# A two-pass chunk of the first layer, a bank shared by ScalarE and VectorE, a three-pass sum over d, and the late weights in 26 parts

## What is computed

```python
e = jnp.stack([tbl_0[ids[:, 0]], ..., tbl_38[ids[:, 38]]], axis=1)   # (1024, 39, 16)
x0 = xk = e
outs = []
for W in (f0, f1, f2):                         # (39*39,128), (128*39,128), (128*39,128)
    z = jnp.einsum('bfd,bgd->bfgd', x0, xk).reshape(b, f * g, d)
    xk = jnp.einsum('bpd,pm->bmd', z, W)       # x1, x2, x3
    outs.append(xk)
z = jnp.sum(jnp.concatenate(outs, axis=1), axis=-1)     # sum over d: r1, r2, r3
h = jnp.concatenate([z, dense_ctx], axis=1)             # 400 columns
h = jnp.maximum(h @ W_top1 + b_top1, 0.0)               # 512
h = jnp.maximum(h @ W_top2 + b_top2, 0.0)               # 256
y = h @ W_top3                                          # 1
```

## Time and profile before

| | us |
|---|---|
| median of 3 timed runs | 1279.11 |
| lowest and highest of them | 1278.82, 1797.93 |
| the profiled execution's own time | 1282.0 |
| its span, first to last instruction | 1279.9 |
| TensorE busy | 1244.3 (97%) |
| VectorE, GpSimd, ScalarE busy | 1056.1, 951.3, 752.1 |
| mean granted TensorE clock | 0.999 |

### The profile page before, as it was taken

The page is one execution under the profiler, slowest core; times in us unless marked ns, Lnnn a source line. Parts: engine busy times, 40 slices in busy tenths (PEclk is TensorE's granted clock), DMA queues, the critical chain, the costliest instruction groups (busy, mean ns, idle before and its releaser), DMA issues.

```text
span 1279.9 us, 19975 instructions
## 1 busy us (share of the span) xinstructions
PE 1244.3 (97%) x5517; PEld 969.6 (76%) x5517; DVE 1056.1 (83%) x3366; ACT 752.1 (59%) x2426; POOL 951.3 (74%) x844
## 2 busy tenths in 40 slices
PE   1989999999999999999999999999999999999999
PEld 0667778777787778777787777877787777877766
DVE  4778996988869997899878888699977989688882
ACT  4556664666646665566646666466655666566652
POOL 7668886788858886788867888588877888665650
PEclk9999999999999999999999999999999999999999
DMA  7542222122222212122211222222121222111000
GB/s 169 158 130 59 68 69 54 38 67 61 65 61 68 61 47 54 51 66 68 70 46 44 65 60 65 66 62 51 48 69 49 68 69 69 39 50 49 3 1 1
DMA packets 121764, 78.69 MB, mean 61 GB/s; under 512 B 77436, under 2 KB 89826, under 8 KB 121652
## 3 DMA queue, kind: packets, MB, share of 16 engines
q1 hardware_dynamic: 107418, 73.69, 20.4%
q0 software_dynamic: 10240, 2.64, 2.6%
q10 hardware_dynamic: 3994, 1.09, 0.4%
HBM read 18.50 MB, written 2.63 MB: 17 GB/s over the span
## 4 chain that ended last, share of the span: by engine, by line
PE 92%; SPq 3%; DMA 2%; POOL 1%; issue 1%; DVE 0%; ACT 0%
PE ps L510 22%; PE ps L514 22%; PE ps L511 22%; PE ps L490 13%; PE ps L537 6%; PE ps L526 5%; POOL x_in L404 1%; PE ps L602 1%; PE ps L473 1%; DMA x_rows<-x_in 1%; PE ps L614 1%; SPq L323 1%; DMA x_in<-in_tables,row_at 0%; SPq L377 0%; SPq L337 0%
## 5 line engine op out<-in xcount | busy, mean ns | idle before, releaser
L865 DVE SCALAR_TENSOR_TENSOR terms<-ps,x_scal,terms 128x128 f32<-128x128 f32 x2944 | 806.2, 342 | 158.4 <-ACT terms L692 94.1
L692 ACT ACTIVATE terms<-ps,x_scal 128x128 f32<-128x128 f32 x2048 | 583.7, 368 | 372.9 <-PE ps L514 366.0
L428 POOL TENSOR_TENSOR terms<-terms 128x1024 f32<-128x1024 f32 (+2 forms) x384 | 578.1, 1506 | 179.9 <-DVE terms L865 157.3
L510 PE MATMUL ps<-w_high,x_high 128*128 128x512 f32 (+1 forms) x1280 | 582.6, 455 | 4.7 <-DVE x_low L843 2.9
L514 PE MATMUL ps<-w_high,x_low 128*128 128x512 f32 (+1 forms) x1280 | 496.9, 388 | 0.0
L511 PE MATMUL ps<-w_low,x_high 128*128 128x512 f32 (+1 forms) x1280 | 495.1, 387 | 0.0
L404 POOL DMA_INDIRECT x_in<-in_tables,row_at x320 | 304.5, 951 | 81.7 <-issue 66.3
L510 PEld LDWEIGHTS ps<-w_high,x_high 128*128 128x128 f32 x1280 | 241.4, 189 | 85.0 <-issue 20.6
L511 PEld LDWEIGHTS ps<-w_low,x_high 128*128 128x128 f32 x1280 | 241.8, 189 | 77.7 <-issue 29.8
L514 PEld LDWEIGHTS ps<-w_high,x_low 128*128 128x128 f32 x1280 | 240.6, 188 | 50.4
L490 PE MATMUL ps<-prods,w 117*128 117x512 f32 x262 | 135.0, 600 | 5.2 <-DVE prods L831 4.9
(11 more groups left out here) (64 smaller groups left out, 446.8 us busy)
## 6 DMA issues: line engine op xcount, KB each, us to landing
prods<-x_cols SPq DMA_DIRECT2D x189, 234.0 KB
x_cols<-x_rows SPq DMA_DIRECT2D x96, 78.0 KB
x_first<-x_cols SPq DMA_DIRECT2D x95, 78.0 KB
x_in<-in_tables,row_at POOLq DMA_INDIRECT x320
x_diag<-x_scal SPq DMA_DIRECT2D x256, 9.8 KB
x_rows<-x_in SPq DMA_DIRECT2D x32, 80.0 KB, 2.4
s<-in_f SPq DMA_DIRECT2D x3, 832.0 KB, 11.7
wt<-in_W_top SPq DMA_DIRECT2D x1, 768.0 KB, 12.8
```

The source lines that it names most:

```text
L428: nc.gpsimd.tensor_tensor(t[:, 0:n], t[:, 0:n], t[:, n:2 * n], ALU.add).then_inc(s_tree, 1)
L510: nc.tensor.matmul(y, x1_high[:, par, at:at + P], high, start=True, stop=False)
L692: op = nc.scalar.activation(terms[:, u % 2, FB * ACT_BANKS.index(q) + i, :], ps[:, (BANKS * u + q) % RING, i * G:(i + 1) * G], ACT.Copy, s ...
L865: nc.vector.scalar_tensor_tensor(out=acc, in0=y, scalar=x0, in1=acc, op0=ALU.mult, op1=ALU.add).then_inc(s_mac, 1)
```

## The change

Six things change together. (1) The chunk with only two shifts (REST, now chunk 1; SHIFT_OF renames the shifts) is no longer multiplied in full precision. Its 78 rows of highs and, one third at a time, its two times 39 rows of lows lie together in `rest` (117 rows), and two float32r passes with two sets of weights (w0_rest) give what the three passes of a split chunk give. The lows get there by two transfers on ACT's queue (move_rest), the second only after the first pass has read the first. (2) Bank 2 is shared: ScalarE scales it in place in PSUM and VectorE adds all 512 columns to the running sums with one instruction (add_shared), in four chains in place of two. (3) The sum over d takes three float32r passes: x2 and x0 are split into highs and lows (split_x2_high on ACT, split_x2_low and split_scalars on DVE), and the diagonal is moved with both. (4) f2 and the MLP weights are loaded in 26 parts, four behind each group's diagonal, and group 0's diagonal goes out before group 1's rows. (5) In tiles 1 and 2 the passes over chunks are put in other slots, and chunks 5 and 4 change places (CIN1_OF). (6) In the tail the new splits stand among the MLP's.

```diff
+SHARED, ADD_AT = 2, 4
+SCALED_BANKS = tuple(sorted(ACT_BANKS + (SHARED,)))
-CHAINS = 2
+CHAINS = FB
+SHIFT_OF = (0, KT - 1) + tuple(range(1, KT - 1))
+REST, SPLIT = 1, (2, 3, 4)
+X2_HIGH, X2_LOW = 7, 8
+MOVE_LOWS = ((0, 8), (1, 3))
-CIN1 = ((0, 6), (1, 1), (1, 8), (2, 6), (2, 9), (3, 2), (3, 4))
+CIN1 = ((0, 6), (1, 3), (1, 9), (2, 1), (2, 4), (2, 8), (3, 1), (3, 4))
+CIN1_OF = (0, REST, REST, 2, 3, 5, 4, 6)
...
+        def move_rest(queue, i):
+            queue.dma_start(rest[KH:KR, :].bitcast(F32), prods_low[i * F:(i + 1) * F, 0, :].bitcast(F32)) \
+                .then_inc(s_rest, 16)
...
             def move_diag(gf, j):
-                sp.wait_ge(s_scal, gf + 1)
+                sp.wait_ge(s_scl, gf + 1)
                 sp.wait_ge(s_s3, gf * TILES - TILES + CREDIT_S3)
...
                 move_diag(gf, j)
+                for n in range((gf - 1) * 4, min(gf * 4, W2_PARTS + 13)):
+                    load_late(n)
...
+                elif k == REST:
+                    pe.wait_ge(s_wrest, 32)
+                    pe.wait_ge(s_rest, (gf - 1) * 32 + half * 16 + 16)
+                    passes = ((w0_rest[:, half, :], rest[:, :]),)
...
-                nc.tensor.matmul(ps[:, S3_BANK, 0:TB * FX], x2[:, u % 2, :],
-                                 x0_diag[:, j % 2, t].rearrange("p b f -> p (b f)"),
-                                 start=True, stop=True).then_inc(s_s3, 1)
+                nc.tensor.matmul(s3_sum, x2_high[:, :], high, start=True, stop=False)
+                nc.tensor.matmul(s3_sum, x2_high[:, :], low, start=False, stop=False)
+                nc.tensor.matmul(s3_sum, x2_low[:, :], high, start=False, stop=True).then_inc(s_s3, 1)
...
+                        y if q == SHARED else terms[:, u % 2, FB * ACT_BANKS.index(q) + i, :], y, ACT.Copy,
...
+            def split_x2_high(bt, u):
+                act.wait_ge(s_x2, bt * STEPS + u + CREDIT_X2)
+                act.wait_ge(s_s3, bt * STEPS + u - 1 + CREDIT_S3)
+                nc.scalar.activation(x2_high[:, :], x2[:, (u - 1) % 2, :], ACT.Copy).then_inc(s_x2h, 1)
...
+                    if front and now == MOVE_LOWS[0]:
+                        act.wait_ge(s_low, (gf - 1) * (NS + 1) + 1)
+                        move_rest(act, 0)
+                    if front and now == MOVE_LOWS[1]:
+                        act.wait_ge(s_cin1, gf * SLOTS + REST_SLOTS[0] + 1)
+                        move_rest(act, 1)
...
+            def add_shared(bt, u):
+                dve.wait_ge(s_ya, bt * (STEPS * NA) + scaled_through(BANKS * u + SHARED) + CREDIT_A)
+                dve.wait_ge(s_mac, bt * (STEPS * MACS) + added_through(BANKS * u + SHARED) - 1 + CREDIT_MAC)
+                acc = terms[:, u % 2, 0:FB, :].rearrange("p t g -> p (t g)")
+                nc.vector.tensor_tensor(acc, ps[:, (BANKS * u + SHARED) % RING, :], acc, ALU.add).then_inc(s_mac, 1)
```

More of the change, by code:

```diff
@@ L62 @@
 ACT_BANKS = (0, 3, 5, 7)
-NA = len(ACT_BANKS)
-DVE_BANKS = tuple(q for q in range(BANKS) if q not in ACT_BANKS)
-MACS = sum(min(FB, F - FB * q) for q in DVE_BANKS)
-CHAINS = 2
-TERMS = NA * FB
+SHARED, ADD_AT = 2, 4
+SCALED_BANKS = tuple(sorted(ACT_BANKS + (SHARED,)))
+NA = len(SCALED_BANKS)
+DVE_BANKS = tuple(q for q in range(BANKS) if q not in SCALED_BANKS)
+DVE_ORDER = tuple(k for q in DVE_BANKS for k in ((SHARED, q) if q == ADD_AT else (q,)))
+DVE_OPS = {q: 1 if q == SHARED else min(FB, F - FB * q) for q in DVE_ORDER}
+MACS = sum(DVE_OPS.values())
+CHAINS = FB
+TERMS = len(ACT_BANKS) * FB
 W1_CHUNKS = 3
@@ L331, in move_diag, with put_diag @@
+            def put_diag(j):
+                for b in range(TB):
+                    at = slice(b * D, (b + 1) * D)
+                    sp.dma_start(x0_diag[at, j % 2, :, :, b, 0:F].bitcast(F32), x0_hl[at, :, :, :].bitcast(F32)) \
+                        .then_inc(s_diag[j % 2], 16)
             def move_diag(gf, j):
[L333 removed]
+                sp.wait_ge(s_scl, gf + 1)
                 sp.wait_ge(s_s3, gf * TILES - TILES + CREDIT_S3)
[L335 to L338 removed]
+                put_diag(j)
@@ L340, in move_seconds @@
             def move_seconds(gf, j):
-                for k in range(1, KT):
-                    sp.wait_ge(s_cin1, gf * KT - KT + k + 1)
-                    move_second(sp, k, j)
+                for n in range(1, SLOTS):
+                    sp.wait_ge(s_cin1, gf * SLOTS - SLOTS + n + 1)
+                    if n != REST_SLOTS[0 if gf == 1 else 1]:
+                        move_second(sp, CIN1_OF[n], j)
             def next_cols(gf, j):
@@ L488, in cin1 @@
                     passes = ((w0[:, k, :], prods[0:KR, k, :]),)
-                for n, (w, x) in enumerate(passes):
-                    mm = nc.tensor.matmul(ps[:, X1_BANK, :], w, x, start=(k == 0 and n == 0),
-                                          stop=(k == KT - 1 and n == len(passes) - 1))
+                for i, (w, x) in enumerate(passes):
+                    mm = nc.tensor.matmul(ps[:, X1_BANK, cols], w, x, start=(k == 0 and i == 0),
+                                          stop=(n == SLOTS - 1 and i == len(passes) - 1))
                 mm.then_inc(s_cin1, 1)
@@ L555, in prologue @@
                 pe.wait_ge(s_denl, len(DENSE_BANKS))
-                for k in range(KT):
-                    cin1(0, k, True)
-                pe.wait_ge(s_w0h, NS)
-                pe.wait_ge(s_w0l, NS)
+                for n in range(SLOTS):
+                    cin1(0, n, True)
+                pe.wait_ge(s_w0h, NS + 1)
+                pe.wait_ge(s_w0l, NS + 1)
                 pe.wait_ge(s_w1h, len(W1_PIECES))
@@ L906, in step @@
                     if q in DVE_BANKS:
+                        if q == ADD_AT:
+                            add_shared(bt, u)
                         mac(bt, u, q)
+                    if q == X2_LOW and bt + u > 0:
+                        split_x2_low(bt, u)
+                    if front and now == SPLIT_SCALARS:
+                        split_scalars(gf, j)
                     if front and now in PRODUCTS:
```

196 lines of the change are left out of this document (133 added, 63 removed).

## The result

The changed kernel takes 1260.04 us (median of 4, 1259.3 to 1261.18). The kernel before has a median of 1280.43 over four runs. One of the four, at 1797.93, was a slow run and is left out of the ratio; the median of the others is 1279.11. The ratio is 0.985, 95% interval 0.984 to 0.986: some 19 us faster, in the range of 1246 to 1272 and 6 us above the forecast. The profiled execution took 1261.18 us for a span of 1259.4.

The account below looks back on a forecast made before the run. TensorE's queue of passes was taken as the bound. 1282.0 − 27.0 + 3.1 − 2.5 + 0.6 + 0.9 = 1257.1 us profiled; with the timed median 2.9 lower, the forecast is 1254 us, range 1246 to 1272.

Parts of the forecast that it names:

- Passes, −27.0: TensorE: sum over d in three 320-wide passes saves 14.3 us; two single passes on the remaining chunk save 12.7.
- rival D: TensorE's sum over d: three passes cost as much as before (0.519), 11 us less gain, 1265 us; chance 0.09.
- Rival B: TensorE: new passes run closer than today's single passes and no wait appears; gains 30.9 us, time 1247; chance 0.12.
- Waits at tiles 1 and 2, +3.1: TensorE waiting for the lows' two transfers or bank 9's space: margins 0 to 0.7 us, charged 0.1 a group.
- Rival A: Transfers of the lows land late, 0.4 to 0.8 us a group: 1263 to 1276, say 1268; chance 0.24.
- GpSimd, no cost: GpSimd's x2, needed sooner by ScalarE's split behind bank 7, still comes in time with about 1 us left.
- Start, −2.5 and +0.6: Weights in pieces save 2.5 us (bounds −3.4 and +2); two more ScalarE instructions before the first factor cost 0.6.
- Tail, +0.9: ScalarE waits for the last x2 before storing the first h1, mostly covered; the following splits cost 0.9 us.
- VectorE's 33.0 a group: VectorE's work per group rises from 32.07 to 33.0 us, of a group of 34.44.
- Rival C: VectorE becomes the bound at bank 1, the add and bank 4 in every step: 1334 us at worst; chance 0.05.
- ScalarE's 970 us: Sign to look for: ScalarE's busy time over the run rises to about 970 us.
- the cheap bound: ScalarE's 128-wide PSUM-writing activates taken as long as SBUF-writing ones, 0.285 us; twice that would add 1.4 us a group.

Follow-up runs that it names:

- the passes one slot earlier: The changed kernel with both passes on the remaining chunk one bank earlier, behind banks 2 and 8 of tile 1: 1269.71 us, ratio 0.993.
- the first diagonal: The changed kernel with group 0's diagonal and the two w0_rest transfers issued by ScalarE, not SP: 1259.74 us, ratio 0.985.

## Why the prediction was right, and where it was off

The mechanism was right: TensorE's passes set the time, and what the changed kernel gains comes from them. Of the other terms three were mis-sized, and they cancel in part. Against the profiled 1261.18, where the sum gave 1257.1:

- **Passes, −27.0.** A group went from 35.30 to 34.40 us, predicted 34.44; over 31 groups −27.6 to −27.9. The three passes of the sum over d take 0.45, near the forecast's 0.432, so rival D falls; how the gain divides between chunk and sum over d wasn't run apart. Rival B falls too: the nine passes from 736.43 to 738.51 take 0.231 each. By the Trainium skill, "TensorE: Matmul & The Clock Gate", section "Back-to-back issue gap", a 320-wide pass would take 0.136 by an estimate; the rows have 0.15. This section of the Trainium skill gives that formula for a pass by itself, and for a stream 131 ns a pass at 512 columns. The 0.231 us of this stream agrees with neither.
- **Waits at tiles 1 and 2, +3.1: none in a steady group.** The step that failed is the time of the two issues: the prediction lets an issue begin when the activates ahead of it are done ("ScalarE reaches the issue at about T1 + 0.3, behind bank 7 and the x2 copy"; the second "behind bank 3 of tile 1, about T1 + 5.0"). Below is the changed kernel, with tile 1 starting at 678.11. The first issue comes 0.2 before that, 0.03 after VectorE's split of the lows has ended (677.89, where the prediction put it), and the x2 copy ahead of it in the program starts later. The second comes 3.2 after it, 0.03 after the chunk's first pass has ended (681.27), while bank 3's activates ahead of it start at 681.92. In all 31 groups both issues come 0.03 to 0.04 after what they wait for. The clause "during which no later instruction is handed on" is not what failed; the runs bear it out (the last section). Rival A was close all the same: one slot earlier, and the wait is there (the passes one slot earlier, above).

```profile
677.10 1.14 ACT L766 ACTIVATE terms<-ps,x_scal 128x128 f32<-128x128 f32 x4 [0.36 <-PE ps L576]
...
677.21 0.68 DVE L930 TENSOR_TENSOR prods_low<-prods,rest 78x512 fp32r<-78x512 f32 x1
...
677.91 0.79 ACTq L314 DMA_DIRECT2D rest<-prods_low  x1
...
678.11 0.33 ACT L775 ACTIVATE x_high<-x 128x128 fp32r<-128x128 f32 x1
...
681.30 0.78 ACTq L314 DMA_DIRECT2D rest<-prods_low  x1
...
681.92 2.19 ACT L766 ACTIVATE terms<-ps,x_scal 128x128 f32<-128x128 f32 x8
```

- **GpSimd, no cost: +4.9 in the profile (0.7 in seven batches), 5.8 by experiment.** This is the largest part of what made the forecast too low: "If VectorE ends 0.9 later, about 1 us is left. No cost." It is true of the group that it was read from, and false for the one group of a batch in which GpSimd also renumbers. The trace of the kernel before shows that group too, and nobody had to wait there yet:

```profile
692.54 0.27 POOL L399 TENSOR_TENSOR row_at<-ids_now,ids_base 128x40 uint32<-128x40 uint32 x1 [1.53 <-DMA x_in<-in_tables,row_at]
692.89 4.92 POOL L428 TENSOR_TENSOR terms<-terms 128x1024 f32<-128x1024 f32 x3
697.89 0.46 POOL L432 TENSOR_TENSOR x<-terms 128x128 f32<-128x128 f32 x1
```

- **Start, −2.5 and +0.6: about +0.4.** Bank 9 of the second batch's first step begins at 191.53 us, where it was 194.06: −2.5, of which the passes are −3.6 and the renumbering +0.7. The parts are larger than the sum. The 3.68 us wait for a factor, is gone as forecast, and more came back than its bound of −3.4: that step took 12.35 and takes 7.37, where the same step of other groups went from 8.69 to 7.37, so 3.7. TensorE's own wait is only about half of it. Behind that wait the granted clock fell to 0.50, the level of 1.2 GHz, for some 3.4 us, and the passes started 0.43 apart; they count as busy, so of the window in the earlier trace rows the 68.57 of 72.00 don't show it, only the mean clock of 0.98 does, and the prediction has no term for it. Half the clock for 3.4 us is some 1.7 us (an estimate). It belongs to this one execution: its mean clock is 0.999, and the 31 runs of the kernel before that were timed beside the experiments all have 1.000. Kernel before:

```profile
87.75 0.50 PE L510 MATMUL ps<-w_high,x_high 128*128 128x512 f32 x1 [1.83 <-DVE terms L865]
```

```profile
89.00:92.00 3.00, 3.00 (x8) 2.35 (x8) 3.00 (x13) 0.38 (x2) 1.22 (x2) 0.50 0.43 116
```

  Loading in parts is worth 4.0 by experiment. Against it, bank 9 of the first step begins at 48.50 in place of 46.81, and the step behind it takes 9.95, 2.6 more than the same step of other groups. So "the diagonal of group 0 now stands ahead of group 1's factors" was priced too low by the profile; the timed runs don't confirm it (the first diagonal, above). In the changed kernel its eight issues hold SP's queue 7.16 us, group 1's rows go out at 37.24 in place of 33.84, and TensorE waits at 50 us for what comes of them and at 57 for the first lows:

```profile
30.04 7.16 SPq L377 DMA_DIRECT2D x_diag<-x_hl  x8
37.24 0.59 SPq L287 DMA_DIRECT2D x_rows<-x_in  x1
```

```profile
50.19 1.13 PE L552 MATMUL ps<-prods,w 117*128 117x512 f32 x2 [1.00 <-ACT x_scal L732]
...
56.76 0.47 PE L552 MATMUL ps<-rest,w_rest 117*128 117x512 f32 x1 [0.67 <-DMA rest<-prods_low]
```

- **Tail, +0.9: +1.1.** As forecast from the earlier trace rows, ScalarE stores the first h1 behind a wait of 5.09 us for the last x2:

```profile
1217.30 0.31 ACT L775 ACTIVATE x_high<-x 128x128 fp32r<-128x128 f32 x1 [5.09 <-POOL x L483]
1217.52 1.25 ACT L860 ACTIVATE w_high<-ps,bt 128x512 fp32r<-128x512 f32 x2
```

Together 1282.0 − 27.6 + 4.9 + 0.4 + 1.1 = 1260.8, within 0.4 of the profiled time. From there to the median the forecast took off 2.9; here it is 1.1. The fall of the clock in the profiled execution of the kernel before can account for most of that difference.

VectorE's 33.0 a group became 32.1, and its idle time before the multiply-adds fell from 158.4 to 116.7 us, not below 100. (The prediction calls the 158.4 its idle time in the whole run; that was 1279.9 − 1056.1 = 223.8, and is 195.8 now.) Rival C was far off: in the kernel without the shared bank VectorE is busier, and TensorE doesn't wait for it. ScalarE's 970 us became 911.2. The two issues don't explain that, since the 970 leaves them out already (752.1 + 31 × 7.0). The new rows are as long as forecast (142.7 and 43.2, and 21.1 and 11.2 for the copies of the chunk and of x0: 218 us), but activates that follow one another overlap, starting 0.25 apart while each lasts 0.34 to 0.40, and what overlaps counts once. Its PSUM-writing activates are the cheap bound: 343 ns. The rows agree with the lock of which the Trainium skill, "SBUF — State Buffer", section "Who interferes with whom", tells (L935 takes 0.68 alone, 0.776 in the mean and 1.26 at 685.10, beside the tree), but none shows TensorE held up by it: behind that 1.26 VectorE stood idle 0.55.

## What to carry to other kernels

Where a result becomes due sooner, look at its maker in every kind of step, also in the one that does the work of once a batch; a margin read from one regular group isn't the margin. With TensorE at 97% a pass taken away is worth its full time only where the next wait is further off than the pass is long, so look for it before you count on the gain. An edit that costs nothing by itself, as the exchange of two passes, can carry all the others: 27 us here.
